# Second cross attention: score products and mask on four 64x64 quarters of the array, two banks a tile, and one output bank

## What is computed

```python
def _L1_xattn_ref(x, context, mask, W_q, W_k, W_v, W_o, b_o):   # HEADS 8, DIM_HEAD 64
    q = (x @ W_q).reshape(b, n, HEADS, DIM_HEAD)
    k = (context @ W_k).reshape(b, j, HEADS, DIM_HEAD)
    v = (context @ W_v).reshape(b, j, HEADS, DIM_HEAD)
    sim = jnp.einsum('bihd,bjhd->bhij', q, k) * scale
    ...   # masked places of sim get the most negative number, softmax over j, times v, times W_o, plus b_o
```

## Time and profile before

| | us |
|---|---|
| median of 3 runs | 257.46 |
| lowest, highest | 256.94, 261.43 |
| span of the profiled execution | 255.3 |
| TensorE busy | 239.0 |
| VectorE busy | 175.9 |
| ScalarE busy | 141.8 |
| GpSimd busy | 77.9 |

### The profile page before, as it was taken

One profiled execution on the slowest core, in us unless ns is written; L12 is line 12 of the kernel. 1 busy time (PEld: TensorE's weight loads), 2 busy tenths in 40 slices (PEclk: granted clock), 3 DMA queues, 4 the chain that ended last, 5 costly groups with the idle time before them and its releaser, 6 DMA issues.

```text
span 255.3 us, 5508 instructions
## 1 busy us (share of the span) xinstructions
PE 239.0 (94%) x1993; PEld 163.9 (64%) x1994; DVE 175.9 (69%) x602; ACT 141.8 (56%) x293; POOL 77.9 (31%) x137
## 2 busy tenths in 40 slices
PE   8988899998999999999999886999998999999995
PEld 8555577774535766756593534678887566577775
DVE  5465699874878836445217979957655688889975
ACT  0764776764264688467657445465565744544540
POOL 7856900001040474667465051533401000000000
DMA  5888960178100000000000000000000000000002
GB/s 136 173 196 245 302 152 0 31 220 205 44 1 0 1 3 0 0 1 3 0 1 3 1 0 0 3 3 3 3 5 0 3 0 0 1 3 0 0 3 82
DMA packets 24040, 11.64 MB, mean 46 GB/s; under 512 B 13017, under 2 KB 23006, under 8 KB 24014
## 3 DMA queue, kind: packets, MB, share of 16 engines
q1 hardware_dynamic: 22973, 10.94, 16.5%
q0 software_dynamic: 80, 0.20, 0.7%
q10 hardware_dynamic: 960, 0.16, 0.3%
HBM read 8.68 MB, written 2.62 MB: 44 GB/s over the span
## 4 chain that ended last, share of the span: by engine, by line
PE 73%; DVE 15%; ACT 5%; issue 3%; POOL 2%; DMA 1%; DVEq 0%; POOLq 0%; ACTq 0%
PE bank L1029 10%; PE bank L1041 10%; PE bank L897 6%; PE bank L884 6%; PE bank L916 6%; PE bank L776 3%; DVE stats L1720 3%; PE bank L1014 3%; PE bank L758 2%; PE bank L976 2%; PE bank L648 2%; PE bank L792 2%; PE bank L693 2%; PE bank L986 2%; PE bank L999 2%
## 5 line engine op out<-in xcount | busy, mean ns | idle before, releaser
L516 POOL TENSOR_TENSOR X<-X,att 128x128 f32<-128x128 f32 x72 | 30.4, 457 | 29.2 <-ACT att L1469 29.1
L441 POOL TENSOR_TENSOR rs<-rs,halves 128x4 f32<-128x4 f32 x14 | 14.9, 1063 | 61.8 <-DVE rs L1735 61.1
L1029 PE MATMUL bank<-XT,Wb 128*128 128x512 f32 x64 | 29.9, 599 | 0.0
L1041 PE MATMUL bank<-Wb,att 128*128 128x128 f32 x224 | 27.2, 278 | 0.0
L1041 PEld LDWEIGHTS bank<-Wb,att 128*128 128x128 f32 x224 | 26.1, 192 | 1.4 <-issue 1.4
L1905 DVE SCALAR_TENSOR_TENSOR att<-bank,cols,att 128x512 f32<-128x512 f32 x18 | 13.5, 749 | 16.8 <-ACT att L1458 7.8
L1469 ACT ACTIVATE att<-bank,comb 128x128 f32<-128x128 f32 x72 | 20.2, 383 | 6.9 <-PE bank L916 6.8
L1509 ACT ACTIVATE att<-bank 128x512 f32<-128x512 f32 x32 | 18.7, 599 | 9.7 <-PE bank L1029 9.7
L916 PEld LDWEIGHTS bank<-W2a,att 128*128 128x128 f32 x144 | 18.0, 192 | 5.0 <-issue 3.6
L916 PE MATMUL bank<-W2a,att 128*128 128x128 f32 x144 | 18.7, 276 | 0.0
L884 PE MATMUL bank<-XT,W1a 128*128 128x512 f32 x36 | 18.2, 595 | 0.0
(11 more groups left out here) (229 smaller groups left out, 484.1 us busy)
## 6 DMA issues: line engine op xcount, KB each, us to landing
Wb<-in_L_ffn_W SPq DMA_DIRECT2D x1, 1024.0 KB, 5.5
Wb<-in_L_ffn_W SPq DMA_DIRECT2D x8, 128.0 KB, 5.2
X<-in_x SPq DMA_DIRECT2D x2, 256.0 KB, 3.1
k_scratch<-QKVT SPq DMA_DIRECT2D x1, 512.0 KB, 3.9
q_scratch<-QKVT SPq DMA_DIRECT2D x1, 512.0 KB, 4.7
Wb<-k_scratch SPq DMA_DIRECT2D x1, 512.0 KB, 4.6
v_scratch<-QKVT SPq DMA_DIRECT2D x1, 512.0 KB, 6.1
V<-q_scratch SPq DMA_DIRECT2D x1, 512.0 KB, 6.2
```

The source lines that it names most:

```text
L441: nc.gpsimd.tensor_tensor(rs[:, 0, cut], rs[:, 1, cut], halves[:, :], ALU.pow).then_inc(l_root[h], 1)
L516: nc.gpsimd.tensor_tensor(X[:, h * HT + t, :], X[:, h * HT + t, :], part0[:, i % 2, t, :], ALU.add).then_inc(f_acc, 1)
L1029: mm(bank[i % 4][:, :], W1b[:, e, f * P:(f + 1) * P], XT[:, half(h)], start=True, stop=True).then_inc(m_up, 1)
L1041: last = mm(bank[4 + h][:, t * P:(t + 1) * P], hid[:, e % 2, f, tile], W2b[:, e, f, :], start=(f == 0), stop=(f == F1 - 1))
```

## The change

Three things in the functions. The score products go to all four pairings of row half `h2` and column half `j` (head pair `2 i + j`). Since the two row halves now write the same partitions, they write different banks: a tile takes banks `2 (t % 2) + h2`, 256 columns in each. The two banks of a tile are one tensor (`twin`), so that VectorE still reads a tile with one instruction. The mask is four products, each of 64 rows of ones; `maskrow` now has all 128 partitions, and its constant is 64 times smaller. The transposed probabilities move to bank 4, the value products to banks 5 and 6, and the output product always takes bank 7. `project_out(t)` so waits for the addition of tile `t - 1`. `transpose_xn(5, 0)` goes to bank 0, and has a wait.

The orders of all engines are written anew, from the first product to the last, and the expert loop of TensorE and ScalarE is written out. Below are the functions, and of the orders the parts that the text speaks of.

```diff
-        bank = [ctx.enter_context(nc.psum_tensor(f"bank{i}", [P, 512], fp32)) for i in range(8)]
+        twin = [ctx.enter_context(nc.psum_tensor(f"bank{2 * i}", [P, 2, 512], fp32)) for i in range(2)]
+        bank = [twin[i // 2][:, i % 2, :] for i in range(4)]
+        bank += [ctx.enter_context(nc.psum_tensor(f"bank{i}", [P, 512], fp32)) for i in range(4, 8)]
...
-        maskrow = sb("maskrow", [1, N], bf16)
+        maskrow = sb("maskrow", [P, N], bf16)
...
-            return 5 if t < HT else (5, 7)[t % 2]
+            return 7
...
+                if n == 5 and h == 0:
+                    pe.wait_ge(c_sub, NT - 1)
+                if n == 5 and h == 1:
+                    pe.wait_ge(c_otc, 2 * NT)
...
-                dst = bank[t % 2]
-                bias = per_col(maskrow[0:1, t * P:(t + 1) * P], NHP)
-                mm(dst[:, :], onesb[0:1, :], bias, start=True, stop=False, skip_group_check=True)
-                for hp in range(NHP):
+                for h2 in range(2):
+                    rows = slice(h2 * S, (h2 + 1) * S)
+                    bias = per_col(maskrow[rows, t * P:(t + 1) * P], NHP // 2)
+                    for j in range(2):
+                        mm(bank[2 * (t % 2) + h2][j * S:(j + 1) * S, 0:2 * P], onesb[rows, 0:S], bias,
+                           start=True, stop=False, skip_group_check=True)
+                for i in range(NHP // 2):
                     for b2 in range(2):
-                        for h2 in range(2):
-                            tok = slice(t * P + b2 * S, t * P + (b2 + 1) * S)
-                            last = mm(dst[h2 * S:(h2 + 1) * S, (2 * hp + b2) * S:(2 * hp + b2 + 1) * S],
-                                      Q1T[h2 * DH1:(h2 + 1) * DH1, hp, tok], K1T[h2 * DH1:(h2 + 1) * DH1, hp, tok],
-                                      start=False, stop=(hp == NHP - 1), skip_group_check=True)
+                        tok = slice(t * P + b2 * S, t * P + (b2 + 1) * S)
+                        for j in range(2):
+                            for h2 in range(2):
+                                rows, hp = slice(h2 * DH1, (h2 + 1) * DH1), 2 * i + j
+                                last = mm(bank[2 * (t % 2) + h2][j * S:(j + 1) * S, (2 * i + b2) * S:(2 * i + b2 + 1) * S],
+                                          Q1T[rows, hp, tok], K1T[rows, hp, tok],
+                                          start=False, stop=(i == NHP // 2 - 1), skip_group_check=True)
                 last.then_inc(c_scores, 1)
...
             def project_out(t):
                 pe.wait_ge(c_otc, 2 * t + 2)
-                if 1 <= t <= HT:
+                if t == 0:
+                    pe.wait_ge(c_qc[1], 4)
+                else:
                     pe.wait_ge(c_added, t)
-                if t == HT + 1:
-                    pe.wait_ge(c_qc[1], 4)
-                if t > HT + 1:
-                    pe.wait_ge(c_added, t - 1)
...
             def subtract_max1(t):
                 dve.wait_ge(c_scores, t + 1)
-                s = bank[t % 2][:, :].rearrange("p (a s) -> p a s", s=S)
-                then(V.tensor_reduce(sm[:, t, 0, :], s, AX.X, ALU.max))
+                s = twin[t % 2][:, :, 0:2 * P].rearrange("p h (a s) -> p h a s", s=S)
+                then(V.tensor_reduce(sm[:, t, 0, :].rearrange("p (h a) -> p h a", h=2), s, AX.X, ALU.max))
```

TensorE's order in the attention, and the experts' beginning of it after:

```diff
             transpose_xn(4, 1, 6)
+            queries1(1, 0)
+            queries1(1, 1)
+            queries1(1, 2)
+            queries1(1, 3)
+            transpose_probs1(0)
             scores1(3)
-            queries1(1, 0)
-            transpose_probs1(0)
-            queries1(1, 1)
+            scores1(4)
             weigh_values1(0)
             transpose_probs1(1)
-            queries1(1, 2)
-            queries1(1, 3)
+            scores1(5)
+            weigh_values1(1)
             project_out(0)
             transpose_probs1(2)
-            scores1(4)
-            weigh_values1(1)
-            scores1(5)
+            project_out(1)
+            transpose_probs1(3)
             weigh_values1(2)
-            transpose_probs1(3)
-            project_out(1)
             scores1(6)
             weigh_values1(3)
+            project_out(2)
             transpose_probs1(4)
-            project_out(2)
+            project_out(3)
+            weigh_values1(4)
             scores1(7)
-            weigh_values1(4)
-            project_out(3)
             transpose_probs1(5)
             project_out(4)
+            weigh_values1(5)
             transpose_probs1(6)
-            weigh_values1(5)
+            project_out(5)
+            weigh_values1(6)
             transpose_probs1(7)
-            weigh_values1(6)
-            project_out(5)
-            transpose_xn(5, 0, 6)
+            project_out(6)
             weigh_values1(7)
-            project_out(6)
+            transpose_xn(5, 0, 0)
             project_out(7)
...
             up1(0, 0, 1)
             up1(0, 1, 1)
...
+            up1(1, 0, 0)
+            count(0)
+            up1(1, 1, 0)
+            up1(1, 0, 1)
+            count(1)
+            down1(0, 1)
+            count(2)
```

429 lines of the change are left out of this document (253 added, 176 removed).

## The result

The changed kernel takes 259.95 us (median of 20 runs, 257.25 to 261.94), the kernel before 257.42 (20 runs, 256.94 to 261.43). The ratio is 1.006, 95% interval 1.003 to 1.009. So it is slower by a little over half a per cent, which is within 2%; the forecast was 256.3, range 253.1 to 259.2. (The ratio leaves out executions more than 1.5% above the kernel's fastest, the medians don't; that is why it is smaller than the quotient of the medians.)

The account below looks back on a forecast made before the run. TensorE and VectorE nearly level in the second cross attention, so handoffs and orders decide. 0.0 - 0.75 - 0.7 + 0.15 + 0.2 = -1.1, with 0.06 from the walk -1.2: 257.46 to 256.3 us, range 253.1 to 259.2.

Parts of the forecast that it names:

- A score tile: Second cross attention, TensorE: slot falls from 1.19 to 0.82 us, saving 0.37 a tile, 2.2 over six tiles.
- Rival (d): VectorE's reading of two banks is dearer by 0.15 an instruction, 2.4 us in all: 257.5, chance 0.06.
- Rival (c): The array's quarters don't overlap, score slot up to 1.26 or 1.07 us: 257.8, chance 0.08.
- The walk of the attention: Second cross attention's new orders followed slot by slot: TensorE's saving returns as idle time, costed at 0.0.
- rival b: Second cross attention: single output bank makes each `project_out` wait for the previous addition, 1.45 a link: 258.4, chance 0.16.
- -0.75 for `widen(0, 1)`: Before the second cross attention: `widen(0, 1)` behind `down0(1, 8)` starts the latter and VectorE's moments 0.75 us sooner.
- the rest: Reordered first attention (0, 1 us either way), first cross attention (+0.2), first experts, `widen_queries` (+0.15) and `mask_row`.
- -0.7 for the search: Routing search: `count(0)` after three `up1`, not four; last products start at 248.15 against 248.87.
- Head and first cross attention, +0.35: `widen_queries` later before the first scores, +0.15; gate's weights later in the first cross attention, +0.2.
- (b) and half of (d): High end of the range: output bank chain plus half the dearer two-bank reading, put at 259.2.
- (b) twice over: Output bank loss doubled, taken as what slower beyond 2% needs: 262.6, chance 0.04.
- Rival (a): Second cross attention: TensorE keeps its saving of 6 x 0.37 = 2.2 us: 254.1, chance 0.22.

Follow-up runs that it names:

- e5: Changed kernel with unread filler products at all four places where profiles showed half clock, and its own fillers moved back: 257.63 us.
- e6: e5 with `add_bias(0)` moved back behind `weigh_probs(0)` on GpSimd: 256.98 us.
- e10: e6 with `transpose_xn(3, 0)` and its copy back in the old places, `scores1(7)`, `probs1(5)`, `subtract_max1(7)` earlier, five fillers there removed: 256.12 us.
- e14: e10 with the first experts' second half in the old order on all four engines, `widen(0, 1)` staying behind `down0(1, 8)`: 255.48 us.
- e2: Changed kernel with eight unread products, five ahead of `transpose_xn(4, 0)` and three between it and the queries: 259.59 us.
- e13: e12 with only `widen(0, 1)` moved behind `down0(1, 8)`: 257.28 us.
- e12: Kernel before with 16 unread filler products in its own idle places at 26.5, 148, 154 and 158: 257.19 us.
- e4: Changed kernel with 16 unread products ahead of `scores1(0)`, `scores1(2)`, the second queries and `transpose_probs1(5)`: 258.57 us.

## Why the prediction was wrong

The gap is 259.95 - 256.3 = 3.65 us. The runs account for it: clock 2.32 (changed kernel to e5), `add_bias(0)` 0.65 (e5 to e6), order of the first experts 0.64 (e10 to e14), together 3.6. That this closes so well is in part luck: each step is good to about 0.3, the last was measured in a kernel with another tail, and the sum held 0.35 for head and first cross attention that didn't come, against which stands the fillers' own price of about 0.3.

- **The clock** was the step that failed most, and it stands nowhere in the sum: I took the earlier trace rows, all from an execution at clock 1.00, and counted idle time of TensorE as free wherever something else set the end. "2.2 us saved on TensorE come back as idle time of TensorE" was right, and that was the danger. I wrote that the fillers are put together and counted 0.2 for the gate's weights; what they had covered at 59.4 I didn't ask. None of the rivals holds this case. In its place the runs show a clock below 1.00 in all 20 executions, worth 2.3 us. The Trainium skill, "TensorE: Matmul & The Clock Gate" (what's actually happening), says that the array's clock is halved when it has been idle and that the moment isn't tied to the kernel's start. On the moment the runs agree: with the same instructions up to 148 us, the low stretches lay at other places or nowhere from one execution to the next. As to idle, no gap ahead of a drop was longer than 1.43 us (e2), and there were products between the gaps. The page speaks against a change that makes TensorE idle, and belonged among the rivals.
- **A score tile**: forecast 0.82 (products 0.62, mask 0.20), measured 0.60 (0.47 and 0.13). The direction was right, the size too careful: 15 ns an instruction, under the 19 of the earlier trace rows. The chain of handoffs and not the tile set the end, as forecast.
- **Reading two banks in one instruction**: 0.68 for the maxima and 0.69 for the subtraction in the changed kernel, as before. Rival (d) is out. Rival (c) too, by the 0.60.
- **The walk of the attention**: `transpose_probs1(4)` forecast 175.8, measured 176.59; VectorE idle before `add1(3)` 1.37 and 1.38; TensorE idle before `transpose_probs1(5)` 1.1 and 1.33; first `up1` 189.2 and 189.85. `scores1(3)`, forecast 165.2, came at 166.32. In this execution the low stretch held it up, in those at a clock of 1.00 `add_bias(0)` does (166.25 in e5). With `add_bias(0)` moved back (e6) it comes at 165.25 and the first `up1` at 188.96: the walk itself was right. It left GpSimd's queue out, where `add_bias(0)` had moved ahead of `weigh_probs(0)`. I had priced every engine's moved work but this engine's, and taken its duration for a cost only where someone waits for its result.
- **The output bank** (rival b) did what the walk said and no more: 1.38 once. That it could be avoided, e10 shows.
- **-0.75 for `widen(0, 1)`**: wrong in the sum, since `down0(1, 8)` starts at 132.33 (before 132.29). I had costed the one moved instruction and not the reordered nine experts ahead of it, which I put among "the rest". e14 gives 0.64 once their order is the old one.
- **-0.7 for the search**: right. From the first `up1` to the last products 58.85 us (189.85 to 248.70) against 59.61 before; twelve rounds of 1.96 and three of 2.6 to 2.7.
- **Head and first cross attention, +0.35**: the first scores came at 26.24, 0.28 sooner than before and not 0.15 later, and `down0(0, 0)` 0.28 sooner too; it was gone by `down0(0, 1)`, at 87.43 in both. So these terms were 0 rather than +0.35.
- **Three sums off to the side**: (b) and half of (d) is 258.4 + 0.6 = 259.0 and not 259.2; (b) twice over is 256.3 + 4.2 = 260.5 and not 262.6; 230.07 + 3.85 + 7 x 2.2 is 249.3 and not 250.1. None of them enters the forecast.
- **Rival (a)**, TensorE keeping its saving, didn't happen: 3.6 us less busy, the same span. That a better order could keep part of it, e10 shows with 1.0.

Still open: in which executions which of the four places drops, and why the mean clock of one kernel is 0.993 in one run and 0.974 in the next. e13 shows three of twelve runs at 0.993 although it is filled like e12, which had none; its new idle time of 0.38 ahead of `widen(0, 2)` may be the reason, but no run tested it. What each single reorder of the first attention is worth wasn't tried.

## What to carry to other kernels

Where a change shortens TensorE's work and something else sets the end, ask what TensorE will do with the time: in a kernel whose clock falls to 1.2 GHz in some executions, idle time is not free, and a product that nobody reads is cheap cover. Look at the granted clock of many runs, not at one profile; the profiled execution of this kernel was its luckiest. Before moving a filler, a bias addition or another instruction "without cost", note what it covers or blocks where it goes, on GpSimd's queue too. And when a wait comes back one instruction later, stop moving single instructions and look for the chain.

## What the runs showed of the hardware

- 32 instructions of 64 x 64 x 64 on four quarters, into two banks, take 0.47 us, 15 ns each; on two quarters 0.87. The Trainium skill, "TensorE: Matmul & The Clock Gate" (section on 56 ns against 53.3 ns), gives about 25 ns as the least distance between starts; here the mean is less.
- Four mask products of 64 rows, 256 columns, bf16, on four quarters: 0.10 to 0.14 us together.
- A subtraction and multiplication of 128 x 128 elements on VectorE, within SBUF, takes 0.34 us alone, 1.17 beside a running addition of 128 x 512 on GpSimd. Reading a bank beside the same addition costs VectorE nothing: 0.69 with it (changed kernel, 159.37, beside 158.76 to 160.02) as without.
- A low stretch of about 3.4 us costs from nearly nothing (151.2 to 154.6, hidden behind VectorE) to about 1 us (e4: two of them, span 257.2 against 255.2 at 1.00), and more where it is longer (e2: one at 26 and one of twice the length at 162, span 259.2).
